# Expert up projections computed transposed, from weights fetched per tile: graph attention and mixture of experts on one core

## What is computed

```python
flat = _rmsnorm(x, ln2_w).reshape(-1, Cx)
probs = jax.nn.softmax(flat @ router_w.T, axis=-1)
tp, ti = jax.lax.top_k(probs, TOPK)
tp = tp / (jnp.sum(tp, axis=-1, keepdims=True) + 1e-09)
weights = jnp.sum(tp[..., None] * jax.nn.one_hot(ti, NE, dtype=flat.dtype), axis=1)
out = jnp.zeros_like(flat)
for e in range(NE):
    hh = jax.nn.silu(flat @ w1[e].T) * (flat @ w3[e].T)
    out = out + weights[:, e:e + 1] * (hh @ w2[e].T)
return x + out.reshape(Bx, Tx, Cx)
```

## Time and profile before

| | |
|---|---|
| median of 3 runs | 1743.07 us (1736.86 to 1748.71) |
| profiled execution | 1734.74 us, span 1732.9 us, mean granted clock 0.974 |
| PE busy | 1522.1 us, 88% |
| DVE busy | 1388.9 us, 80% |
| ACT busy | 1047.8 us, 60% |
| POOL busy | 902.6 us, 52% |
| DMA moved | 79.02 MB, 46 GB/s on average |

### The profile page before, as it was taken

One profiled execution on the slowest core, in us unless ns is written; L12 is line 12 of the kernel. 1 busy time (PEld: TensorE's weight loads), 2 busy tenths in 40 slices (PEclk: granted clock), 3 DMA queues, 4 the chain that ended last, 5 costly groups with the idle time before them and its releaser, 6 DMA issues. The chain is left out here.

```text
span 1732.9 us, 40746 instructions
## 1 busy us (share of the span) xinstructions
PE 1522.1 (88%) x10930; PEld 1122.0 (65%) x10930; DVE 1388.9 (80%) x4725; ACT 1047.8 (60%) x4091; POOL 902.6 (52%) x722
## 2 busy tenths in 40 slices
PE   3678999999999999999999999999999999987673
PEld 2455677666766677767766677776776677755452
DVE  3678888888888888888888888888898889875441
ACT  2576676666666666666666676666666676653221
POOL 1133555556555555556566555556555555555433
PEclk9889999999999999999999999999999999999897
DMA  5001222222222222222222222222222222222221
GB/s 144 16 27 32 42 39 50 46 49 51 40 47 40 46 47 49 47 49 48 45 41 44 48 49 46 48 51 48 42 48 41 44 49 49 40 42 45 42 33 20
DMA packets 141977, 79.02 MB, mean 46 GB/s; under 512 B 32277, under 2 KB 137405, under 8 KB 141501
## 3 DMA queue, kind: packets, MB, share of 16 engines
q0 software_dynamic: 46208, 34.37, 13.9%
q1 hardware_dynamic: 95549, 42.04, 9.8%
HBM read 33.09 MB, written 43.26 MB: 44 GB/s over the span
## 5 line engine op out<-in xcount | busy, mean ns | idle before, releaser
L462 POOL DMA_INDIRECT out<-ys,xt x264 | 416.3, 1577 | 480.4 <-DMA out<-ys,xt 289.4
L446 POOL DMA_INDIRECT routed<-fx,slot x256 | 258.4, 1009 | 227.1 <-DVE slot L843 159.8
L1128 PEld LDWEIGHTS bank<-w_s,hsT 128*128 128x128 f32 (+1 forms) x1584 | 207.5, 193 | 62.9 <-issue 52.3
L1128 PE MATMUL bank<-w_s,hsT 128*128 (+1 forms) x1584 | 230.3, 282 | 15.3 <-ACT hsT L603 14.6
L545 ACT ACTIVATE p<-ub,nm 128x128 f32<-128x128 f32 x512 | 198.3, 392 | 30.1 <-DVE nm L765 29.9
L1107 PE MATMUL bank<-w_s,xT 128*128 x528 | 204.7, 470 | 4.6 <-DVE xT L905 2.4
L911 DVE SCALAR_TENSOR_TENSOR hg<-sg,bank 128x341 f32<-128x341 f32 x264 | 133.9, 507 | 89.0 <-ACT sg L596 85.8
L1111 PE MATMUL bank<-w_s,xT 128*128 x528 | 200.8, 462 | 0.0
L596 ACT ACTIVATE sg<-bank 128x341 f32<-128x341 f32 x264 | 120.0, 454 | 128.1 <-PE bank L1107 126.1
L602 ACT ACTIVATE hsT<-bank 128x256 f32<-128x256 f32 x264 | 101.7, 385 | 152.2 <-PE bank L1121 148.5
L556 ACT ACTIVATE p<-bank,nm 128x128 f32<-128x128 f32 x512 | 180.2, 365 | 18.3 <-DVE nm L771 17.2
(11 more groups left out here) (166 smaller groups left out, 3354.9 us busy)
## 6 DMA issues: line engine op xcount, KB each, us to landing
xt<-routed SPq DMA_DIRECT2D x264, 65.0 KB, 1.9
xs<-in_x SPq DMA_DIRECT2D x32, 256.0 KB, 3.0
out<-bs SPq DMA_DIRECT2D x32, 256.0 KB, 2.3
out<-ys,xt POOLq DMA_INDIRECT x264
routed<-fx,slot POOLq DMA_INDIRECT x256
w_s<-in_w SPq DMA_DIRECT2D x2, 1364.0 KB
adj<-in_adj SPq DMA_DIRECT2D x32, 64.0 KB, 2.8
w_s<-in_w SPq DMA_DIRECT2D x2, 512.0 KB
```

Of the source, the lines that this page charges most:

```text
L446: pool.indirect_dma_start(routed, bass.IndirectOffsetOnAxis(slot[p][:, i:i + 1], 0), fx[i // GB][p][:, i % GB, :], None).then_inc(S[f"sc{p ...
L462: pool.indirect_dma_start(out_rows, bass.IndirectOffsetOnAxis(xt[r][:, C:C + 1].bitcast(I32), 0), ys[r][:], None, compute_op=ALU.add, **bo ...
L1128: last = pe.matmul(y_p[:, 0:C], hsT[r % 2][0:n, c, :], w2_s[0:n, bass.ds(e, 1), c, :].rearrange("p a c -> p (a c)"), start=c == 0, stop=c ...
```

## The change

- w1 and w3 no longer lie in SBUF for all experts. They are packed side by side in HBM, padded from 341 to 384 (HP) columns each, and SP loads the pair of one expert for each tile (`E.w.r`, 128 partitions of 3072 bytes, 393 KB) into one of three buffers `w13` (WB = 3). The load waits for h3 of the tile three before.
- The up projection turns its operands round: 3 pieces of 128 columns of w1 stationary and xT moving (128 columns), then 3 pieces of w3. So h1, h3, sg, hg and hu come out with the hidden values on partitions, 128 x 384, and the down projection takes hu as its stationary operand directly. The transposes `E.t` and ScalarE's copies to hsT are gone; `E.d.r` now waits for hu of its tile and ys of the tile before.
- The copy of the rows to xT moves from VectorE to ScalarE and multiplies by ln2 there. The factor 0.5 of silu moves into the row weighting (L929, an immediate).
- The value load of the expert's number on TensorE stands behind the up projection. The two loads and scalings of w1 and w3 at the start are gone.
- All lists are written anew.

```diff
-                        sp.dma_start(w1_s[:], w1).then_inc(S["ld_w"], 16)
-                        sp.dma_start(w3_s[:], w3).then_inc(S["ld_w"], 16)
...
+                def load_weights(r):
+                    w = g - 4
+                    k = w * RING + r
...
+                    e = sp.value_load(expert_at(w, p, r), min_val=0, max_val=NE - 1)
+                    if k >= WB:
+                        sp.wait_ge(S["h3"], k - WB + 1)
+                    sp.dma_start(w13[k % WB][:].rearrange("c a n -> c (a n)"),
+                                 w13_h[bass.ds(e, 1)].rearrange("e c n -> c (e n)")).then_inc(S[f"wq{k % WB}"], 16)
...
-                    act.activation(hsT[r % 2][:, 0:2, :].rearrange("p a b -> p (a b)"), hs_p[:, 0:256], ACT.Copy)
-                    act.activation(hsT[r % 2][0:HC[2][1], 2, :], hs_p[0:HC[2][1], 256:384], ACT.Copy).then_inc(S["hsT"], 1)
...
+                    act.activation(xT[r % 2][:], x_p[:, 0:128], ACT.Copy, scale=ln2c[:]).then_inc(S["xT"], 1)
...
-                    dve.tensor_copy(xT[r % 2][:], x_p[:, 0:128]).then_inc(S["xT"], 1)
...
                 def up(r):
...
+                    pe.wait_ge(S[f"wq{k % WB}"], 16 * (k // WB + 1))
+                    pe.wait_ge(S["xT"], k + 1)
+                    for c in range(3):
+                        last = pe.matmul(h1_p[:, c * 128:(c + 1) * 128], b[:, 0, c * 128:(c + 1) * 128], xT[r % 2][:], start=True, stop=True)
+                    last.then_inc(S["h1"], 1)
+                    if k:
+                        pe.wait_ge(S["hu"], k)
+                    for c in range(3):
+                        last = pe.matmul(h3_p[:, c * 128:(c + 1) * 128], b[:, 1, c * 128:(c + 1) * 128], xT[r % 2][:], start=True, stop=True)
+                    last.then_inc(S["h3"], 1)
...
-                    for c, (o, n) in enumerate(HC):
-                        last = pe.transpose(hs_p[0:n, c * 128:(c + 1) * 128], hu[r % 2][:, o:o + n], ident[:])
-                    last.then_inc(S["htr"], 1)
...
-                        last = pe.matmul(y_p[:, 0:C], hsT[r % 2][0:n, c, :], w2_s[0:n, bass.ds(e, 1), c, :].rearrange("p a c -> p (a c)"),
+                        last = pe.matmul(y_p[:, 0:C], hu[r % 2][0:n, c, :], w2_s[0:n, bass.ds(e, 1), c, :].rearrange("p a c -> p (a c)"),
```

More of the change, by code:

```diff
@@ L36 @@
 GW = HD + 1
+HP = 384
+WB = 3
 HC = [(0, 128), (128, 128), (256, HID - 256)]
@@ L143, in gnn_moe_block @@
 def gnn_moe_block(nc, x, adj, W, WT, att_src, att_dst, ln1, ln2, wqkv, wo, router,
[L144 removed]
+                  w13_h, w2, rope_h, ident_h, causal_h, before_h, small_h, queue_h, out):
     ctx = ExitStack()
@@ L184, in gnn_moe_block @@
         rout = sb("rout", [C, 128])
-        w1_s = sb("w1_s", [C, NE, HID])
-        w3_s = sb("w3_s", [C, NE, HID])
+        w13 = [sb(f"w13_{i}", [C, 2, HP]) for i in range(WB)]
         w2_s = sb("w2_s", [128, NE, 3, C])
@@ L243, in gnn_moe_block @@
         ys = [sb(f"ys{i}", [128, C]) for i in range(RING)]
-        xT, sg, hu, hsT = two("xT", [C, 128]), two("sg", [128, HID]), two("hu", [128, HID]), two("hsT", [128, 3, 128])
-        hg, ln2h = two("hg", [128, HID]), sb("ln2h", [C, 1])
+        xT, sg, hu = two("xT", [C, 128]), two("sg", [128, HP]), two("hu", [128, 3, 128])
+        hg = two("hg", [128, HP])
         bank = [ctx.enter_context(nc.psum_tensor(f"bank{i}", [128, 512], F32)) for i in range(8)]
@@ L257, in gnn_moe_block @@
         rank_ps base bst0 bst1 sc0 sc1 padsc tabw table
-        last xtr xT h1 h3 htr sg hg hu hsT yp ys
+        last xtr xT h1 h3 sg hg hu yp ys
         zs turn_dve turn_pool turn_pe turn_sp""".split()
-        names += [f"{n}{r}" for n in ("xq",) for r in range(RING)]
+        names += [f"{n}{r}" for n in ("xq",) for r in range(RING)] + [f"wq{r}" for r in range(WB)]
         TABLE = 14
@@ L376, in load_tile @@
                     sp.dma_start(xt[r][:], src).then_inc(S[f"xq{r}"], 16)
-                return {"nx": nx, "f": f, "l": load_tile}
+                def load_weights(r):
+                    w = g - 4
+                    k = w * RING + r
+                    if r == 0:
+                        if is_last(w):
+                            sp.wait_ge(S["last"], 1)
+                        else:
+                            sp.wait_ge(S["table"], w + 1)
+                        sp.sem_inc(S["turn_sp"], 1)
+                    e = sp.value_load(expert_at(w, p, r), min_val=0, max_val=NE - 1)
[3 more added lines that the diff above has]
+                                 w13_h[bass.ds(e, 1)].rearrange("e c n -> c (e n)")).then_inc(S[f"wq{k % WB}"], 16)
+                return {"nx": nx, "f": f, "l": load_tile, "w": load_weights}
             phase1(sp, steps, "sp")
@@ L1088, in turn_x @@
                 def turn_x(r):
-                    if isinstance(g, int) and g == 4 and r == 0:
-                        pe.wait_ge(S["wscale"], 2)
                     pe.wait_ge(S[f"xq{r}"], 2 * k8 + 16)
```

136 lines of the change are left out of this document (58 added, 78 removed).

## The result

The change made the kernel slower: 1783.5 us as a median of 4 runs (1775.7 to 1793.5) against 1741.9 (4 runs), ratio 1.025, 95% interval 1.022 to 1.028. The profiled execution took 1793.5 us, the longest of the four, with a span of 1791.7 and a mean granted clock of 0.956. One execution of a later run (the kernel before with empty instructions) took 6876 us where its other nine took 1736 to 1743; it is left out of that run's ratio, and nothing here explains it.

What follows compares the result with a forecast made beforehand. TensorE was taken as first limit in the steady part, GpSimd's scatter-add chain in the tail. From 1734.7 us, -34 (products) - 29 (waits) + 6 (tail) = -57 gave 1678, as a median 1686, range 1660 to 1705.

Steps and rivals of the forecast that it cites:

- work and waits of the engines: Over the whole kernel, products were to save 34 us and shorter waits of TensorE 29 us.
- Products: On TensorE, six up products take 1.335 us per tile; net -0.145 us per tile, 34 us off over 236 tiles.
- the rival with bare weight loads (1800): TensorE's added weight loads are not hidden in the array: +0.355 us per tile, about 1800 us; chance 0.06.
- Single operations: On ScalarE, scaled copy 365 ns and tanh over 384 columns 490; on VectorE, two operations widen from 507 to 546 ns.
- Waits: TensorE gets back 1.0 of 2.8 us idle per body, over about 29 bodies: -29 us, bounds 0 and -81.
- Arrival of the weights at nothing: A weight load's arrival costs nothing, since two tiles of other work hide it; without that cover 3 us or more per tile.
- The scatter-add at +0.2 us: Beside weight loads each scatter-add slows from 4.18 us by 0.2; +6 us in the tail, 45.2 us of chain per steady period.
- the rival at 4.8: Scatter-adds slow to 4.8 us beside weight loads: 48.1 us per period, -15 and tail +17, about 1745 us; chance 0.12.
- The chain formula: GpSimd's scatter-add chain per steady period: seven steps plus a long eighth, 7 × 4.18 + 14.5 = 43.8 us before the change.
- the rival "no change" with its 0.12: Scatter-adds slowing to 4.8 us cancel the gain: -15 us in the steady part, +17 in the tail, about 1745; chance 0.12.
- the one at 5.1 us: Scatter-adds at 5.1 us make the period 50.2, +46 and +26 us, about 1815, slower; chance 0.08.
- my bound of about 1%: Times within 1% of 1743 us (1726 to 1760) could not be told from no change; chance 0.18.

Runs made afterwards that it cites:

- three shifted kernels: The changed kernel with 40 empty instructions ahead of the loop, on ScalarE, VectorE or TensorE alone: 1729.0, 1728.8 and 1731.4 us, ratios 0.993, 0.995 and 0.995.
- run without bytes: The changed kernel loading only 48 of 768 weight columns per tile (24.6 KB, not 393 KB) from the fourth tile on, products using stale weights: 1649.5 us, ratio 0.949.
- before + traffic: The kernel before plus a 393 KB load of expert weights per tile into three buffers that nothing reads: 1815.7 us, ratio 1.045.
- best version: The changed kernel with weights loaded by DMA from a resident SBUF copy, only the 341 real columns of each half (349 KB per tile): 1677.6 us, ratio 0.965.
- slow SBUF kernel: The changed kernel with 393 KB per tile by DMA from a resident SBUF copy, written as six pieces of 128 columns: 1763.4 us, ratio 1.016.

## Why the prediction was wrong

On a common base of 1737 us for before, the ratios give these terms. Each ratio is known to about 0.003, so each term to some 5 to 8 us, and 0.994 is the mean of the three shifted kernels.

| term | from | measured | forecast |
|---|---|---|---|
| work and waits of the engines | run without bytes, 0.949 | -89 | -63 |
| weight loads beside scatter-adds | 0.994 - 0.949 (before + traffic: 0.045) | +79 (+79) | +6 |
| stall | 1.025 - 0.994 | +53 | none |
| sum | 1.025 | +43 | -57 |

**Products: right.** 1.34 us per tile against 1.335. TensorE's weight loads are hidden: the run without bytes keeps it 97% busy over a period shorter than forecast, which the rival with bare weight loads (1800) can't give. The section of the Trainium skill on which that rival leaned (Perfetto Trace Analysis, Identifying the Most-Contended Engine) names two measures for TensorE, MFU (its useful arithmetic as a share of the peak) and the busy share of weight loads, and the prediction took up the second alone. That share did rise, from 699 of 1000 us before to 810 in the run without the bytes, but the time fell by 5% there.

**Single operations: right.** Scaled copy 367 ns (365), tanh 493 (490), hg 549 and hu 551 (546 each).

**Waits: too small.** I gave back 1.0 of 2.8 us idle per body. Without the bytes the period is 45.42; against 48.8 over the same stretch, less the 1.2 us of the products, 2.2 came back. Much of it hangs on GpSimd's new lists (some 80 us between old and new with the bytes, up to 77 without), whose rows I had shown in the order but not priced. With the old lists and without the bytes the kernel stands at 0.994, and next to nothing of the gain is left.

**Arrival of the weights at nothing: right.** Six buffers gain nothing, and TensorE hardly waits for the loads. The page of the run with ScalarE's code shifted has 12.8 us for it in 264 tiles:

```profile
L1099 PE MATMUL bank<-xT,w 128*128 128x128 f32 x1584 | 232.1, 284 | 24.4 <-DMA w<-in_w_h 12.8
```

**The scatter-add at +0.2 us: this step failed**, twice over. Its size was about 0.45: 4.57 to 4.77 us in the nine tails with 393 KB per tile from HBM, 4.64 on average, against 4.13 to 4.27 in the five with hardly any traffic. That is near the rival at 4.8. And I charged it only to the tail, as 45.2 us of chain stayed under 46.5 of TensorE's period. The chain formula itself held within 1 us where GpSimd seldom waits for anything else and no stall comes in: 7 × 4.76 + 14.2 = 47.5 us for the run with ScalarE's code shifted, whose period is 48.1; 7 × 4.51 + 14.2 = 45.8 for the best version, period 46.4; 7 × 4.49 + 14.3 = 45.7 with half the bytes, period 46.2; 7 × 5.2 + 14.2 = 50.6 with six buffers, period 49.8. (The step is the mean spacing of scatter-adds whose wait ended on the DMA, the last term the long step of a body. In the steady part of the kernel before this step was 4.28 us; I had put in the 4.18 of its tail.) Had I put 4.7 into my own formula, it would have said 7 × 4.7 + 14.5 = 47.4 us, 1.2 less than 48.6: with 28 × 0.45 = 13 us in the tail, 1735 - 35 + 13 = 1713, as a median 1722, against 1729 to 1731 for the three shifted kernels. They are the rival "no change" with its 0.12 (ratio 0.993 to 0.995). The changed kernel itself fell between that rival and the one at 5.1 us, but for another reason, the stall. I had argued that a scatter-add itself moves the same 128 rows; that says nothing of what it stands beside.

The Trainium skill, DMA: Bandwidth & Descriptors, section Queues, rings and completion order, has each DMA engine change between queues only at the end of a packet. Scatter-adds are slower beside the loads, which fits, but no run here shows in which order an engine serves the two queues. The 512-byte pieces don't test the rule either: the Trainium skill's packet gathers several descriptors, while the profile counts every piece. What the runs do show is that cutting the load into 302237 pieces in place of 133277 left the step at 4.70 us against 4.71 to 4.77. The source mattered more: 4.32 to 4.44 us in the tail beside the same bytes from SBUF.

**The stall: in no rival.** It turns "no change" into "slower": my bound of about 1% hides 0.994, but not 1.025. Nothing in the profile of before could have priced it. The chain takes it in as well: its long step grows from 14.2 to 16.0 us, 7 × 4.73 + 16.0 = 49.1 of the 50.3.

What stays open is the mechanism. Shown is that it comes and goes with a shift of any of three engines' code, in kernels whose work, order and packets are the same; that ScalarE and VectorE resume within 0.06 us of each other in it, in ten of the 12 bodies from 600 to 1200 us of the slow SBUF kernel; and that both wait for signals of TensorE that come late and together. What holds the signals back is not shown. A wait for a block of instructions finds no support: of the 12 ScalarE stalls over 1.9 us from 600 to 1200 in the changed kernel, 3 have a packet of the instruction queues (q8 and q14 of the page) starting in them or in the microsecond before, no more than chance would give. One rival stands untested. The five traces with the stall are also the five with gaps in their semaphore records: the changed kernel has 3975 such records of VectorE for 4481 signals that its instructions send, while in the other fifteen none is short. Each time here comes with the span and clock of its own execution, so all were recorded, and the stall may come from the recording or the gaps from the stall; no run tells. Open as well is how much of the 77 us that the old GpSimd lists cost without the bytes is the stall.

## What to carry to other kernels

When an indirect scatter-add chain waits for its own landing, it is an engine: write its period (steps times latency, and the rest) beside that of the busiest one, and put every new transfer's effect on its latency into it before counting a gain on TensorE. Resident data is better re-copied from SBUF than fetched again from HBM, if it must move at all. Before a loss or gain of 2 to 4% is put down to an edit, look for idle times with nothing pending, and run the kernel again with its code shifted. Do so in every run that is compared: two kernels can have the same time, one by the stall and one by slower transfers, as three and six buffers have here.

## What the runs showed of the hardware

- 40 empty instructions ahead of a loop changed a kernel from 1783 to 1729 us (on any of three engines) and another from 1763 to 1686 (on ScalarE), and a third, the kernel before, not at all (on ScalarE, ratio 1.001).
- In the kernels that gained, TensorE's semaphore signals had come up to 3 us after the modelled end of their products, several within 0.2 us of each other (four within 0.16 us at 850.6 us of the changed kernel), while the products had started at their usual pace. In the fifteen traces without the stall, 3 or fewer of over 2200 signals came over 0.5 us late.
- A 393 KB load per tile of 4.6 to 6 us slows 128-row scatter-adds in the tail from 4.2 us to between 4.57 and 4.77 when it reads HBM, and to between 4.32 and 4.44 when it reads SBUF. Half the bytes from HBM give 4.39. With six buffers the steps that end on their DMA are 5.2 in the steady part, with three 4.7.
- The size of the pieces, 512 or 3072 bytes, made little difference to it: 4.60 us in the tail against 4.57 to 4.72 in the changed kernel, 4.64 against 4.68 beside the kernel before.
- A DMA of rows contiguous at both ends, written as six pieces, ran as one: 134317 packets either way.
